# Two attention and mixture-of-experts layers in one kernel: the second attention's paddings written by ACT in the routed units instead of by POOL, and seven of eight shared units in front of the routed ones instead of six

## The chip, the cores and the metric

The kernel runs on one NeuronCore of a Trainium2 chip. A core has five engines with a queue each: TensorE (PE in the profile) for matrix products, VectorE (DVE), ScalarE (ACT), GpSimd (POOL) and SyncE (SP, which here only issues transfers). They wait for each other by semaphores. The metric is the time on the device in microseconds (us); lower is better.

## The reference

Four blocks follow each other on x of 2 x 512 x 256 float32, each as `x = x + layernorm(block(layernorm(x)))`. Blocks 0 and 2 are attentions (the first linear, with 32 heads of 64; the second with softmax, 32 query and 8 key/value heads of 8). Blocks 1 and 3 are the mixtures of experts (MoE) that the change is about, cut to what they compute:

```python
x = hidden_states.reshape(-1, Dm)                 # 1024 tokens of 256
logits = x @ router_w                             # 8 experts
expert_idx = jnp.argmax(logits, axis=-1)
score = jax.nn.sigmoid(jnp.max(logits, axis=-1))
xs = x * score[:, None]
for e in range(n_experts):
    m = (expert_idx == e)[:, None]
    xe = jnp.where(m, xs, 0.0)
    h = jax.nn.silu(xe @ gate_w[e]) * (xe @ up_w[e])
    out = out + jnp.where(m, h @ down_w[e], 0.0)
shared = jax.nn.silu(x @ shared_gate_w) * (x @ shared_up_w) @ shared_down_w
return out + shared
```

## The kernel before

Everything stays in SBUF as 8 tiles of 128 tokens (NT = 8), apart from the rows that are sorted by expert through memory. Each engine's program is written out by hand, and the order in each queue is the order of the code.

A MoE block (l = 0 for block 1, l = 1 for block 3; `pe_moe`, `act_moe`, `dve_moe`, `pool_moe`, `sp_moe`) works like this. TensorE makes the router's logits, VectorE chooses an expert and a slot for each token, and POOL scatters the tokens' rows to `sorted_x` with eight indirect transfers (L618). VectorE then works out which expert each tile of 128 sorted rows belongs to, in a chain of small operations that ends with the casts `row` (L937) and `expert` (L939). SP reads `row` and fetches 15 tiles of sorted rows (NR = NT + E - 1 = 15) into `xg`, a ring of 8. TensorE reads `expert` and multiplies each tile by its expert's weights. Each routed tile of results is stored by POOL with an indirect transfer (L624); at the end SP loads all results as `y`, VectorE adds the shared expert's part `y_shared`, and the statistics and normalisation of the next block follow.

The products are made in NU = 23 units u, 15 routed and 8 shared (the shared expert on one of the 8 token tiles). Units 0 to NSF - 1 are shared, the next 15 routed, the rest shared again. With NSF = 6, units 6 to 20 are routed, 21 and 22 shared. A unit passes through these stages:
- routed only: TensorE transposes the rows (`turn_rows`, L1306) and ACT copies them (L1059)
- gate/up on TensorE (L1282 shared, L1289 routed)
- SiLU on ACT (L1046), the product h on VectorE (L865 shared, L867 routed)
- transposes of h on TensorE (`turn_h`, L1298), copied by ACT (L1052)
- down on TensorE (L1318), copied from PSUM by VectorE (L876) to `y_shared` or to a ring `yr` of 4, from which POOL stores.

Step i of the loop holds gate/up of unit i, the transposes of h of unit i - 1, the row transposes of the routed tile two units ahead (both of the first two in step NSF - 1), and down of unit i - 2. The last gate/up step changes places with the transposes of h before it, and the step behind the last routed unit holds two downs:

```python
            for i in range(3, NU + 1):
                if i == NU - 1:
                    turn_h(i - 1)
                if i < NU:
                    gate_up(i)
                if i != NU - 1:
                    turn_h(i - 1)
```

The h product just ahead of the chain of small operations is unit 2's (`gated(2)`); the h products of units 3 and on stand behind `expert`.

The second attention (block 2) keeps its heads in tiles with padded columns: `qs` and `ks` (32 columns a head, of which 24 to 31 are zero, or one at three of them in `ks`, before the row maxima are put in) and `vals` (a column of ones for the softmax's sum, zeros behind). `pool_l1` writes these paddings in block 1: POOL issues eight memsets behind its scatters, five of zeros with no wait between them, then three of ones. `L1_CONSTS` is the number of signals that ACT, VectorE and POOL wait for before they use the tiles in block 2. Between block 1 and block 2 TensorE runs `keep_warm(25, 2)` (L1128), 25 products that nobody uses, once the first y is made, and `keep_warm(5, 2)` when VectorE's statistics are there.

Of the kernel before, what the change touches and what calls it, by code (L numbers as in the profile page):

```python
# [25 lines left out]
ACT = mybir.ActivationFunctionType  # L26
AX = mybir.AxisListType

P = 128
B, S, D = 2, 512, 256  # L30
NT = B * S // P
TB = S // P
# [14 lines left out]
E, F = 8, 256  # L47
FC = F // P
NR = NT + E - 1
NSF = 6  # L50
NXG = 8
NU = NT + NR
REGION = B * S
# [3 lines left out]
def routed(u):  # L57

    return u - NSF if NSF <= u < NSF + NR else None


def shared_tile(u):
    return u if u < NSF else u - NR

NQ, NKV, HD = 32, 8, 8
# [3 lines left out]
HW = 32  # L71
NKT = B * NKV // GH
Q_AT, K_AT, LO_AT = (0, 1), (0, 2), (2, 1)
MAXAT, MAXN = 3 * HD, 3
VW = 32
# [4 lines left out]
def build(nc, a, out):  # L80
    ctx = ExitStack()
    with ctx:
        def sem(name):
            return ctx.enter_context(nc.semaphore(name))

        def at(name, shape, dt, where):

            n = 1
            for d in shape[1:]:
                n *= d  # L90
            size = n * (2 if dt == BF16 else 4)
            t = nc.alloc_sbuf_tensor_at(name, shape, dt, offset=where[0])
            where[0] += (size + 31) // 32 * 32
            assert where[0] <= LIMIT, (name, where[0], LIMIT, here[0])
            return t
# [16 lines left out]
        ones = at("ones", [P, P], F32, here)  # L112
# [26 lines left out]
        zeros = at("zeros", [P, D], F32, here)  # L139
# [41 lines left out]
        h = [at(f"h{i}", [P, F], F32, me) for i in range(2)]  # L181
# [28 lines left out]
        qs = [at(f"qs{b}", [P, TB, NQ, HW], F32, l1) for b in range(B)]  # L210
        ks = [at(f"ks{b}", [P, TB, NKV, HW], F32, l1) for b in range(B)]
        vals = at("vals", [P, NT, NKV, VW], F32, l1)
# [22 lines left out]
        consts = sem("consts")  # L235
# [49 lines left out]
        l1_consts, l1_ordered = sem("l1_consts"), sem("l1_ordered")  # L285
# [172 lines left out]
        N_CONSTS = 14  # L458
# [74 lines left out]
            nc.gpsimd.tensor_tensor(shift[of][:, sl], nmean[of][:, sl], rstd[of][:, sl],  # L533
                                    ALU.mult).then_inc(rstd_ready[of], 1)

        def pool_l1(pool):

            g = nc.gpsimd
            g.memset(vals[:], 0.0).then_inc(l1_consts, 1)
            for b in range(B):  # L540
                g.memset(ks[b][:, :, :, MAXAT:HW], 0.0).then_inc(l1_consts, 1)
                g.memset(qs[b][:, :, :, MAXAT:HW], 0.0).then_inc(l1_consts, 1)
            pool.wait_ge(l1_consts, 5)
            for b in range(B):
                g.memset(ks[b][:, :, :, MAXAT:MAXAT + MAXN], 1.0).then_inc(l1_consts, 1)
            g.memset(vals[:, :, :, HD:HD + 1], 1.0).then_inc(l1_consts, 1)

        L1_CONSTS = 8

        def order_heads(pool):  # L550

            g = nc.gpsimd
            pool.wait_ge(l1_loaded, 48)
            rows = [(wqkv[:, c], wqkv_in[:, c]) for c in range(KC)] + [(bqkv[:], bqkv_in[:])]
            for to, src in rows:
                for s_ in range(2):
                    cols = slice(s_ * NQ // 2 * HD, (s_ + 1) * NQ // 2 * HD)
                    g.tensor_copy(to[:, cols].rearrange("p (h r d) -> p r h d", r=GH, d=HD),
                                  src[:, cols].rearrange("p (r h d) -> p r h d", r=GH, d=HD)).then_inc(l1_ordered, 1)
                g.tensor_copy(to[:, NQ * HD:], src[:, NQ * HD:]).then_inc(l1_ordered, 1)  # L560
# [41 lines left out]
        def pool_moe(pool, l):  # L602
            g = nc.gpsimd

            g.iota(xn_id[:, :, D:D + 1].bitcast(U32), pattern=[[P, NT], [0, 1]], base=SORTED,
                   channel_multiplier=1).then_inc(numbered, 1)
            pool.wait_ge(numbered, l + 1)
            pool.wait_ge(zeroed, 32 * (l + 1))
            for half in range(2):
                sl = slice(half * TB, (half + 1) * TB)  # L610
                pool.wait_ge(xn_ready[half], (2 * l + 2) * TB)
                pool.wait_ge(score_ready[l], half + 1)
                g.tensor_scalar(xn_id[:, sl, D + 1:D + 2], half_score[:, sl].unsqueeze(2), 0.5, 0.5, ALU.mult,
                                ALU.add).then_inc(score_put[l], 1)
                pool.wait_ge(score_put[l], half + 1)
                pool.wait_ge(slot_ready[l], half + 1)
                for t in range(half * TB, (half + 1) * TB):
                    g.indirect_dma_start(sorted_x[l][:, :], bass.IndirectOffsetOnAxis(ap=slot[:, t:t + 1], axis=0),  # L618
                                         xn_id[:, t, :], None).then_inc(scattered[l], 16)
            if l == 0:  # L620
                pool_l1(pool)
            for r in range(NR):
                pool.wait_ge(yr_ready[l], NSF + r + 1)
                g.indirect_dma_start(routed_y[l][:, :], bass.IndirectOffsetOnAxis(  # L624
                    ap=xg[r % NXG][:, D:D + 1].bitcast(U32), axis=0), yr[r % 4][:], None).then_inc(yr_stored[l][r % 4], 16)
            if l == 0:
                order_heads(pool)
# [330 lines left out]
        def scalar_program(act):  # L958
# [23 lines left out]
            def complete(p):  # L982

                for t in range(NT):
                    if p == BLOCKS - 1:
                        act.wait_ge(last_summed, t + 1)
                        act.wait_ge(rstd_ready[1], 2 * (2 * p + t // TB + 1))
                    nc.scalar.activation(x[:, t, :], x[:, t, :], ACT.Identity,
                                         bias=shift[1][:, t:t + 1]).then_inc(x_summed, 1)
# [44 lines left out]
            turn(3, 0)  # L1034
            turn(3, 1)
            act_moe(act, 1, turn)
            complete(BLOCKS - 1)

        def act_moe(act, l, turn):
            def silu(u):  # L1040
                act.wait_ge(gu_made[l], u + 1)
                if u >= 2:
                    act.wait_ge(h_ready[l], u - 1)
                r = routed(u)
                kw = {} if r is None else dict(scale=xg[r % NXG][:, D + 1:D + 2])
                nc.scalar.activation(sg[u % 2][:], ps[2 + u % 2][:, 0:F], ACT.Silu, **kw).then_inc(silu_ready[l], 1)  # L1046

            def copy_h(u):
                act.wait_ge(hT_made[l], u + 1)
                if u >= 2:  # L1050
                    act.wait_ge(d_made[l], u - 1)
                nc.scalar.activation(hT[u % 2][:], ps[4 + u % 2][:, 0:F].rearrange("p (c n) -> p c n", c=FC),  # L1052
                                     ACT.Copy).then_inc(hT_ready[l], 1)

            def copy_rows(r):
                act.wait_ge(xgT_made[l], r + 1)
                if r >= 2:
                    act.wait_ge(gu_made[l], NSF + r - 1)
                nc.scalar.activation(xgT[r % 2][:], ps[r % 2][:, 0:D].rearrange("p (c n) -> p c n", c=KC),  # L1059
                                     ACT.Copy).then_inc(xgT_ready[l], 1)  # L1060

            def score(half):
                sl = slice(half * TB, (half + 1) * TB)
                act.wait_ge(best_ready[l], half + 1)
                nc.scalar.activation(half_score[:, sl], best[:, sl], ACT.Tanh, scale=0.5).then_inc(score_ready[l], 1)

            act.wait_ge(logits_made[l], 1)
            nc.scalar.activation(lgT[0][0:HC, :], ps[LOGIT_BANK[0]][0:HC, 0:2 * P], ACT.Copy).then_inc(lgT_ready[l], 1)
            silu(0)
            score(0)  # L1070
            silu(1)
            turn(2 * l + 1, 2)
            turn(2 * l + 1, 3)
            copy_h(0)
            copy_h(1)
            score(1)
            silu(2)
            for i in range(3, NU + 1):
                if i == NU - 1:
                    copy_h(i - 1)  # L1080
                if i < NU:
                    silu(i)
                if i != NU - 1:
                    copy_h(i - 1)
                for r in rows_at_unit(i):
                    copy_rows(r)

        def downs_at(i):

            last = NSF + NR - 1  # L1090
            return [i - 2] if i <= last else [last - 1, last] if i == last + 1 else [i - 1]

        def rows_at_unit(i):

            return [0, 1] if i == NSF - 1 else [i + 2 - NSF] if NSF <= i and i + 2 - NSF < NR else []

# [370 lines left out]
        def act_l1(act, normalise, turn_copy, complete):  # L1467
# [11 lines left out]

            act.wait_ge(l1_consts, L1_CONSTS)  # L1480
            for t in range(TB):
# [29 lines left out]
        def pool_l1_loop(pool, link):  # L1511
            g = nc.gpsimd
            pool.wait_ge(l1_consts, L1_CONSTS)
            for t in range(TB):
# [204 lines left out]
        def dve_l1(dve, link, mark, settle, y_tiles, close_stats, sum_x):  # L1719
            v = nc.vector  # L1720
            dve.wait_ge(l1_ordered, L1_ORDERED)
            dve.wait_ge(l1_consts, L1_CONSTS)

# [104 lines left out]
```

## Time and profile before

| | |
|---|---|
| median of 3 runs | 671.64 us (670.51 to 672.01) |
| the profiled execution | 669.68 us |
| its span in the trace | 667.8 us |
| mean granted TensorE clock | 0.986 |
| busy TensorE, VectorE, ACT, POOL | 92%, 61%, 49%, 32% |
| block 1 (MoE, l = 0) | about 254 to 350 us |
| block 3 (MoE, l = 1) | about 577 us to the end |

The profiled execution is one run under the profiler; all rows are from it. The share of an engine's busy time is over the whole span, and says little about a single stage. The granted clock is the share of full speed that TensorE was given: 1.00 is 2.4 GHz and 0.50 is 1.2 GHz. Ends of matrix products are modelled, so two that follow each other may overlap by up to 0.2 us in the rows; starts are the better measure.

### The profile page before, as it was taken

Reading aid. Unit: us, or ns where it says so; the run is one execution under the profiler, and the core shown is the slowest. Engines: PE = TensorE matmul, PEld = TensorE weight load, DVE = VectorE, ACT = ScalarE, POOL = GpSimd, SP = SyncE. Lnnn points to the kernel's source line nnn. Section 1 sums busy time; section 2 is a strip of 40 time slices with the busy share of each in tenths; the row PEclk is TensorE's granted clock in tenths of the full one; section 3 lists DMA queues with packets and bytes.
Section 4 is the critical chain, followed back from the end, with each engine's and each line's share of the span. In section 5 each row is a group of like instructions: output and inputs, shape, how many; then the busy total and the mean of one; then the engine's idle time right before and its main releaser. Section 6 shows DMA issues by size and latency. Waiting matters only on the chain.

```text
span 667.8 us, 11795 instructions
## 1 busy us (share of the span) xinstructions
PE 617.4 (92%) x4298; PEld 408.0 (61%) x4298; DVE 404.4 (61%) x929; ACT 325.1 (49%) x645; POOL 213.2 (32%) x312
## 2 busy tenths in 40 slices
PE   3999999999999988799978999999999999989990
PEld 2887887887888785366665544444444445546660
DVE  4526705632760587533366999989998954743336
ACT  4523423433332224133215589898988875523322
POOL 5870561282073154513333031201010100331331
PEclk9999999999999999899989999999999999999996
DMA  6000200300199992222379994000000000031213
GB/s 220 33 1 33 96 1 20 107 1 1 38 283 299 78 314 77 78 58 81 105 237 346 303 180 3 1 1 2 2 1 2 1 2 1 9 104 55 81 56 126
DMA packets 69000, 57.40 MB, mean 86 GB/s; under 512 B 21520, under 2 KB 64400, under 8 KB 68944
## 3 DMA queue, kind: packets, MB, share of 16 engines
q1 hardware_dynamic: 66736, 50.60, 31.2%
q0 software_dynamic: 2208, 6.05, 2.5%
q8 instruction: 36, 0.59, 0.4%
q14 instruction: 20, 0.16, 0.1%
HBM read 30.78 MB, written 25.85 MB: 85 GB/s over the span
## 4 chain that ended last, share of the span: by engine, by line
PE 73%; DVE 16%; DMA 3%; ACT 3%; issue 2%; POOL 1%; SPq 1%; ACTq 0%; POOLq 0%; DVEq 0%
PE psum L303 9%; PE psum L305 8%; PE psum L304 8%; PE psum L1289 8%; PE psum L1634 8%; DVE mx L1744 7%; PE psum L1606 5%; PE psum L1318 5%; PE psum L1594 5%; PE psum L1619 3%; PE psum L1213 2%; DVE stat L666 2%; PE psum L1564 2%; PE psum L1282 2%; PE psum L1199 1%
## 5 line engine op out<-in xcount | busy, mean ns | idle before, releaser
L1744 DVE TENSOR_REDUCE mx<-psum 128x1 f32<-128x512 f32 x256 | 157.6, 681 | 17.6 <-PE psum L1606 17.5
L1505 ACT ACTIVATE pr<-psum 128x512 f32<-128x512 f32 x256 | 138.0, 598 | 27.9 <-PE psum L1619 26.1
L1634 PE MATMUL psum<-pr,vals 128*32 128x256 f32 x1024 | 77.6, 389 | 0.0
L1619 PE MATMUL psum<-qT,kT 32*128 32x512 f32 x256 | 76.6, 494 | 0.7 <-ACT pr L1505 0.7
L1606 PE MATMUL psum<-kT,qT 32*128 32x512 f32 x256 | 67.7, 488 | 1.7 <-ACT qT L1472 0.7
L1289 PE MATMUL psum<-w_gu,xgT 128*128 x120 | 56.4, 592 | 0.0
L624 POOL DMA_INDIRECT routed_y<-yr,xg x30 | 28.7, 958 | 86.1 <-DVE yr L876 85.5
L1606 PEld LDWEIGHTS psum<-kT,qT 32*128 32x128 f32 x256 | 26.3, 181 | 43.9 <-issue 21.4
L1546 POOL CAST mp<-mx 128x16 bf16<-128x16 f32 x16 | 3.1, 196 | 150.5 <-DVE mx L1744 150.5
L867 DVE SCALAR_TENSOR_TENSOR h<-psum,xg,sg 128x256 f32<-128x256 f32 x30 | 14.5, 484 | 49.8 <-ACT sg L1046 49.8
L1046 ACT ACTIVATE sg<-psum,xg 128x256 f32<-128x256 f32 x30 | 14.2, 474 | 60.4 <-PE psum L1289 60.4
L1013 ACT ACTIVATE q<-psum 128x512 f32<-128x512 f32 x32 | 19.1, 597 | 48.9 <-PE psum L305 48.9
L1634 PEld LDWEIGHTS psum<-pr,vals 128*32 128x32 f32 x1024 | 22.2, 108 | 29.8 <-issue 17.8
L585 POOL TENSOR_TENSOR ksum_t<-k_hi 128x1024 f32<-128x1024 f32 x8 | 19.2, 2401 | 64.6 <-DVE k_lo L814 64.4
L1619 PEld LDWEIGHTS psum<-qT,kT 32*128 32x128 f32 x256 | 34.4, 181 | 8.9 <-ACT pr L1505 4.0
L1019 ACT ACTIVATE q_hi<-q 128x512 fp32r<-128x512 f32 x32 | 20.2, 633 | 40.1 <-DVE q L845 40.1
L303 PE MATMUL psum<-kvo_hi,q_hi 128*128 128x256 f32 x128 | 38.0, 297 | 1.9 <-POOL q_lo L599 1.9
L531 POOL TENSOR_TENSOR rstd<-var,mhalf 128x4 f32<-128x4 f32 x16 | 16.5, 1028 | 64.8 <-DVE nmean L676 64.8
L304 PE MATMUL psum<-kvo_lo,q_hi 128*128 128x256 f32 x128 | 36.1, 282 | 0.0
L305 PE MATMUL psum<-kvo_hi,q_lo 128*128 128x256 f32 x128 | 36.1, 282 | 0.0
L819 DVE TENSOR_TENSOR nk<-psum,same_head 128x8 f32<-128x8 f32 x16 | 1.9, 161 | 53.0 <-PE psum L1191 53.0
L814 DVE SCALAR_TENSOR_TENSOR k_lo<-psum,k_hi 128x512 fp32r<-128x512 f32 x32 | 22.0, 689 | 18.1 <-ACT k_hi L1007 18.0
(214 smaller groups left out, 1406.6 us busy)
## 6 DMA issues: line engine op xcount, KB each, us to landing
sorted_x<-zeros SPq DMA_DIRECT2D x2, 9088.0 KB, 39.2
w_gu<-in_L_ffn_gate_w SPq DMA_DIRECT2D x16, 256.0 KB, 6.2
w_gu<-in_L_ffn_up_w SPq DMA_DIRECT2D x16, 256.0 KB, 6.3
w_d<-in_L_ffn_down_w SPq DMA_DIRECT2D x16, 256.0 KB, 6.6
xg<-sorted_x SPq DMA_DIRECT2D x30, 129.0 KB, 2.2
wk_f<-in_L_attn_Wk SPq DMA_DIRECT2D x4, 512.0 KB, 5.2
wq_f<-in_L_attn_Wq SPq DMA_DIRECT2D x4, 512.0 KB, 6.0
wv_f<-in_L_attn_Wv SPq DMA_DIRECT2D x4, 512.0 KB, 3.7
```

Of the source, the lines that this page charges most:

```text
L303: nc.tensor.matmul(o, lhs[0], rhs[0], start=start, stop=False, **kw)
L304: nc.tensor.matmul(o, lhs[0], rhs[1], start=False, stop=False, **kw)
L305: return nc.tensor.matmul(o, lhs[1], rhs[0], start=False, stop=stop, **kw)
L624: g.indirect_dma_start(routed_y[l][:, :], bass.IndirectOffsetOnAxis(ap=xg[r % NXG][:, D:D + 1].bitcast(U32), axis=0), yr[r % 4][:], None). ...
L1289: last = mm(ps[2 + u % 2][:], xgT[r % 2][:, c], w_gu[:, bass.ds(experts[r], 1), c, :], start=(c == 0), stop=(c == KC - 1))
L1318: last = mm(ps[6 + u % 2][:, 0:D], hT[u % 2][:, c], w, start=(c == 0), stop=(c == FC - 1))
L1505: nc.scalar.activation(pr[d % 3][:, j], s2_bank(d, j), ACT.Exp, scale=SCALE).then_inc(exp_ready, 1)
L1594: last = nc.tensor.transpose(into[:, t * P:(t + 1) * P], src, ident[:])
L1606: mm(s1_bank(c, j), qT1[n % 2][rows, t * P:(t + 1) * P], kT[n // GH][rows, :], start=True, stop=True).then_inc(s1_made, 1)
L1619: mm(s2_bank(d, j), kT[n // GH][rows, kc * P:(kc + 1) * P], qT2[n % 2][rows, :], start=True, stop=True).then_inc(s2_made, 1)
L1634: last = mm(ps[AV_BANK][j * VW:(j + 1) * VW, cols], vals[:, n // NKV * TB + kc, n % NKV // GH * GH + j, :], pr[d % 3][:, j, cols], start=( ...
L1744: v.tensor_reduce(mx[n % 2][:, t, j:j + 1], s1_bank(c, j), AX.X, ALU.max, negate=True).then_inc(max_read, 1)
```

## The change

`NSF` becomes 7: units 0 to 6 are shared, 7 to 21 routed, 22 shared, in both MoE blocks and on all engines. `pool_l1` is removed. In block 1 ACT writes the paddings with activations that copy a constant (`put`), one piece in each of the units 9 to 15, behind that unit's other work: n = 0 and 1 write the zeros of `qs` (128 x 1024 elements), 2 and 3 those of `vals` (128 x 736), 4 and 5 those and the ones of `ks` (128 x 160 and 128 x 96), 6 the ones of `vals` (128 x 64). That is nine activations, so `L1_CONSTS` becomes 9. The parts of `vals` that are overwritten later are no longer zeroed.

```diff
-NSF = 6
+NSF = 7
...
-        def pool_l1(pool):
-
-            g = nc.gpsimd
-            g.memset(vals[:], 0.0).then_inc(l1_consts, 1)
-            for b in range(B):
-                g.memset(ks[b][:, :, :, MAXAT:HW], 0.0).then_inc(l1_consts, 1)
-                g.memset(qs[b][:, :, :, MAXAT:HW], 0.0).then_inc(l1_consts, 1)
-            pool.wait_ge(l1_consts, 5)
-            for b in range(B):
-                g.memset(ks[b][:, :, :, MAXAT:MAXAT + MAXN], 1.0).then_inc(l1_consts, 1)
-            g.memset(vals[:, :, :, HD:HD + 1], 1.0).then_inc(l1_consts, 1)
-
-        L1_CONSTS = 8
+        L1_CONSTS = 9
...
-            if l == 0:
-                pool_l1(pool)
...
+        def put(act, to, value):
+            src = (zeros, ones)[value]
+            nc.scalar.activation(to, src[:, 0:1].unsqueeze(2).to_broadcast([P, to.shape[1], to.shape[2]]),
+                                 ACT.Copy).then_inc(l1_consts, 1)
+
+        def l1_padding(act, n):
+            heads = "p t h w -> p (t h) w"
+            if n == 0:
+                act.wait_ge(consts, N_CONSTS)
+            if n < 2:
+                put(act, qs[n][:, :, :, MAXAT:HW].rearrange(heads), 0)
+            elif n < 4:
+                put(act, vals[:, (n - 2) * TB:(n - 1) * TB, :, HD + 1:VW].rearrange(heads), 0)
+            elif n < 6:
+                put(act, ks[n - 4][:, :, :, MAXAT + MAXN:HW].rearrange(heads), 0)
+                put(act, ks[n - 4][:, :, :, MAXAT:MAXAT + MAXN].rearrange(heads), 1)
+            elif n == 6:
+                put(act, vals[:, :, :, HD:HD + 1].rearrange(heads), 1)
...
                 for r in rows_at_unit(i):
                     copy_rows(r)
+                if l == 0 and i > NSF + 1:
+                    l1_padding(act, i - NSF - 2)
```

## Rows read from the trace of the kernel before

**Rows 1.** The page's fourth part: shares of the chain that ended last, by engine.

```profile
PE 73%; DVE 16%; DMA 3%; ACT 3%; issue 2%; POOL 1%; SPq 1%; ACTq 0%; POOLq 0%; DVEq 0%
```

**Rows 2.** The chain of waits in the first MoE block: start, duration, what.

```profile
269.32 0.42 DVE h L865
...
272.88 4.73 DVE expert L939
...
283.36 0.44 PE psum L1306 x2
```

**Rows 3.** The chain of waits in the second MoE block.

```profile
588.46 0.42 DVE h L865
...
592.02 0.34 DVE expert L939
...
598.10 0.44 PE psum L1306 x2
```

**Rows 4.** Timeline of POOL, both blocks: start, duration, engine, line, operation.

```profile
272.50 0.96 POOL L618 DMA_INDIRECT sorted_x<-xn_id,slot  x1 [0.30 <-issue]
273.46 1.82 POOL L539 MEMSET vals<- 128x2048 f32 x1
...
276.60 0.97 POOL L542 MEMSET qs<- 128x1024 f32 x1
...
591.42 0.96 POOL L618 DMA_INDIRECT sorted_x<-xn_id,slot  x1 [0.30 <-issue]
```

**Rows 5.** Timeline of TensorE where the routed units start, first and second block.

```profile
281.88 0.38 PE L1298 MATMUL psum<-ident,h 128*128 128x128 f32 x2
...
284.50 1.88 PE L1289 MATMUL psum<-w_gu,xgT 128*128 x4
...
595.46 0.38 PE L1298 MATMUL psum<-ident,h 128*128 128x128 f32 x2
...
598.37 1.03 PE L1318 MATMUL psum<-shared_d,hT 128*128 128x256 f32 x4
599.24 1.88 PE L1289 MATMUL psum<-w_gu,xgT 128*128 x4
```

**Rows 6.** Timeline of the first block's end; idle time and releaser in brackets.

```profile
326.55 1.88 PE L1289 MATMUL psum<-w_gu,xgT 128*128 x4
...
328.27 0.38 PE L1298 MATMUL psum<-ident,h 128*128 128x128 f32 x2
...
328.49 1.03 PE L1318 MATMUL psum<-w_d,hT 128*128 x4
...
328.98 0.48 DVE L867 SCALAR_TENSOR_TENSOR h<-psum,xg,sg 128x256 f32<-128x256 f32 x1 [1.80 <-ACT sg L1046]
...
331.29 1.91 PE L1318 MATMUL psum<-w_d,hT 128*128 x8
...
332.36 0.42 DVE L876 COPY yr<-psum 128x256 f32<-128x256 f32 x1 [0.24 <-PE psum L1318]
...
340.63 7.48 PE L1128 MATMUL psum<-ident 128*128 128x128 f32 x50 [2.53 <-DVE y L953]
...
348.67 1.38 PE L1128 MATMUL psum<-ident 128*128 128x128 f32 x10 [0.57 <-DVE nmean L676]
...
350.86 1.82 PE L1111 MATMUL psum<-ident,xn_id 128*128 128x128 f32 x8 [0.81 <-ACT xn_id L979]
```

**Rows 7.** ACT's strided copies (ns min/median/max), and a SiLU of a routed unit.

```profile
L1457 ACT ACTIVATE ks<-qkv x4: 293/301/309, 356.1 to 358.8; 128x128 fp32r<-128x128 f32 x4
L1457 ACT ACTIVATE qs<-qkv x4: 614/614/615, 356.3 to 359.0; 128x512 fp32r<-128x512 f32 x4
...
292.46 0.47 ACT L1046 ACTIVATE sg<-psum,xg 128x256 f32<-128x256 f32 x1 [2.00 <-PE psum L1289]
```

**Rows 8.** TensorE in two stretches: length, busy (instructions), granted clock, DMA share, GB/s.

```profile
277.60:280.00 2.40, 2.32 (x7) 0.50 0.00 0
...
344.60:345.60 1.00, 1.00 (x8) 0.65 0.90 268
```

## The prediction

> **What bounds the kernel now.** I read the page first, then the chain of waits around each mixture-of-experts (MoE) block, then the timelines of the engines there. The chain is TensorE's for 73% and VectorE's for 16%, and POOL and ACT together have 4% [rows 1]. So an edit on POOL or ACT counts only where TensorE or VectorE waits for it, and an edit of TensorE's order only where it moves a wait.
>
> The kernel runs the same MoE code twice, and only the first run has POOL's paddings in it, so the second is a control. Line the two up at VectorE's h product: 269.32 [rows 2] and 588.46 [rows 3], 319.14 us apart. The cast of `expert` starts at 272.88 and at 592.02, again 319.14 apart. It takes 4.73 us in the first block and 0.34 in the second. The second pair of row transposes, which waits for the rows that SP fetches by the table, starts at 283.36 and at 598.10: only 314.74 apart. So the first block loses 319.14 - 314.74 = 4.40 us at this cast, all of it on the chain, because the first routed gate/up product comes at 284.50 against 599.24, also 314.74 apart [rows 5].
>
> What holds a cast of 16 elements? POOL's timeline [rows 4]: its last scatter runs from 272.50 to 273.46, and behind it five memsets without a wait in between, from 273.46 to 276.60 + 0.97 = 277.57. The cast ends at 277.61, right after the fifth. In the second block the last scatter runs to 592.38 and the cast ends at 592.36. The reader is to see that VectorE's cast comes back when POOL's uninterrupted stretch ends, in both blocks.
>
> The Trainium skill, SBUF — State Buffer, Who interferes with whom, has a rule for this: GpSimd and VectorE share one pair of ports as an exclusive lock, casts and copies can need it, and whoever comes second is blocked for the whole instruction of the other. The trace agrees that the cast is blocked, and differs in the length: one memset's lock would be over at 275.28 and the memsets would have cost 1.82 us of the hold; the trace shows 277.61, after five. What follows if the rest is not the memsets' is the second rival.
>
> **Part 1: POOL's eight memsets go.** With them the cast's hold ends as in the second block. The first block then runs at the second's times less 319.14: -4.40 us at the first routed product. Not all of the hold goes: the scatter stays, and it ends at 273.46, where the second block's less 319.14 would be 273.24. So the cast, and the h product that follows it in order on VectorE and restarts TensorE, may come up to 0.22 later than the control says. The bounds are 0 and 0.22; I take 0.2, since the second block's cast ended with its scatter. POOL itself has only the row stores behind the memsets, which wait for the routed rows, so it gains nothing of its own.
>
> **Part 2: ACT writes the paddings.** Nine activations in seven units of the first block. The nearest rows are ACT's strided copies into the same tiles in the same runs of 8 elements [rows 7]: 0.301 us for 128 elements per partition, 0.614 for 512, so 0.82 ns an element. For `qs` (1024 elements): 0.614 + 512 x 0.00082 = 1.03 us, twice. For `vals` (736): 0.80, twice. For `ks` (160 and 96 elements): about 0.33 + 0.28 = 0.61, twice. For the ones of `vals` (64): 0.25. In all 5.1 us of ACT, one piece per unit, behind that unit's last copy. ACT is idle 2.00 us there in each routed unit before TensorE gives it the next SiLU [rows 7], so I cost it at nothing. Bounds: below, nothing; above, every element at the small row's 0.301/128 = 2.35 ns gives 2.4 us for 1024, 0.4 over the idle time in two units. Behind the piece stand the next SiLU and two copies. The product of SiLU is needed by TensorE only one unit later: it is ready 2.91 us after the gate/up product starts (326.55 to 328.98 + 0.48), and is transposed a routed unit and a gate/up later, (2.81 + 0.22) + 1.72 = 4.75 after that start (part 3). So 1.8 us more of cover stands behind the 2.00, and the upper bound is nothing too. Who waits for the paddings: POOL, VectorE and ACT at the second attention's start, while the last is written in unit 15 of 23.
>
> **Part 3: one shared unit moves ahead of the routed ones, in both blocks.** Its own time on TensorE: 1.72 for gate/up (326.55 to 328.27), 0.22 for the transposes of h, 0.87 for down (598.37 to 599.24) = 2.81 us [rows 5, 6]. What it hides, in the second block: between the transposes of h at 595.46 and down at 598.37 there are 2.91 us, and own work there is one pair of transposes of h and two of rows, 3 x 0.22 = 0.66. So 2.25 us are waiting for rows. The unit fills all of it and sticks out by 2.81 - 2.25 = 0.56: the first routed product goes from 599.24 to 599.80. The rows must be there by then: TensorE comes to the second pair at 598.71, and they were there at 598.10. In the first block, less 319.14, it comes at 279.57 and they are there 5.75 after the cast (277.61 to 283.36), at 273.45 + 5.75 = 279.20: hidden too. So the first block starts its first routed product at 599.80 - 319.14 = 280.66 instead of 284.50: -3.84, with the 0.2 of part 1 it is -3.64.
>
> No instruction is added to a queue: the fetches on SP, the weights and the 15 row stores on POOL keep their order. The fetch ring needs stores only eight rows back, which move with the products.
>
> **The end of a block.** The time that counts is when the last two routed rows leave PSUM, since the stores, the loads of y and the next normalisation hang on them; the shared units behind were hidden by that. Before: last routed product at T = 326.55, downs 19 and 20 from T + 4.74 = 331.29, first copy at 332.36 [rows 6]. After: the unit behind the last routed one is now the last of all, whose step transposes first, then multiplies. TensorE is there at T + 2.81, h is ready at T + 2.91, and with a few hundredths for the semaphore that is 0.15 of waiting (an estimate); then 0.22, 1.72, and the two downs at T + 4.90. That is +0.15 in each block. The final shared down ends far ahead of the loads of y: before, two shared units ended 2.53 us ahead of the restart, now one.
>
> **The sum.** First block -3.64 + 0.15 = -3.49. Second block +0.56 + 0.15 = +0.71. Net -2.78, with bounds -2.98 (no rest of the hold) and -2.76. The profiled execution took 669.68 us (span 667.8, 1.88 outside it): 666.9 by this. The median of the runs is 671.64, 1.96 above it; the difference carries over, so 671.64 - 2.8 = 668.8.
>
> **Rivals.** *The hold stays* (slower, 5%). If the cast waits for something other than memsets, for example the eight scatters' descriptors, only the order changes. Then TensorE in the first block goes on from 281.88 (transposes of h) with 0.22 + 0.87 + 1.72 + 0.22 + 0.44 + 0.87 = 4.34, to 286.22 instead of 284.50: +1.72, +0.15 at the end, and +0.71 in the second block: +2.6, 674.2 us. It decides from a rest of the hold of about 3 us on. Against it: the same scatters stand in the second block, and the cast took 0.34.
>
> *A colder clock in front of the second attention* (4%). With one shared unit less behind, TensorE idles 2.53 + 2.81 = some 5.3 us before its warming matmuls at 340.63. The granted clock already falls in them: of 344.6 to 345.6 seven tenths are still at 1.2 GHz (0.65 granted), so it is back at 2.4 some 4.7 us after the restart; after the stall of the cast it was at 1.2 from 277.6 to 280 [rows 8]. The 50 records took 7.48 us; at 2.4 GHz throughout, 0.11 each, they would take 5.5, wholly at 1.2 GHz 10.9. They have 7.48 + 0.57 before the next ones are due, and 0.81 more stand behind those [rows 6]. With cold stretches as long as seen, up to 4.7 us from the start on, they take 5.5 + 2.35 = 7.8: nothing lost. Only if the clock stayed down throughout: 10.9 - 8.05 - 0.81 + 1.1 for the ten cold ones = 3.1, and +0.3 in all, 671.9. The Trainium skill, TensorE: Matmul & The Clock Gate, What's actually happening, says that the idle state is the throttled one and activity releases it; both rises here agree.
>
> *A part of the hold stays* (6%). If only one memset's length was the memsets' doing and the rest of the hold is the last scatter's own, the cast ends at 277.61 - 1.82 = 275.79. TensorE restarts there instead of at 273.4, 2.4 later than in the forecast, and the rows come at 281.5, hidden by the same shift: -3.84 + 2.4 + 0.15 + 0.71 = -0.6, 671.1 us. For it: the rule above. Against it: the second block's cast was free 0.02 before its scatter's end.
>
> *ACT becomes the bound* (2%): a padding over 3.8 us. At 5 us each for the wide ones it is 4 x 1.2 = +4.8 less 2.8, 673.6; no row is near it.
>
> **Chances and range.** Forecast 82%, with a range of its own of 667.6 to 669.8 (the bounds, and some 0.75 us on either side, half of what the runs before spread), and 1% for what I don't see. The rivals lie above and hold 17%, so this range alone would leave out a little more than 2 in 10; 667.0 to 670.6 allows for twice that spread. I count 0.2% (1.3 us) as what a measurement can tell from no change. Faster: the forecast and the lucky ends of the rivals, 0.84; same: the part of the hold and the clock, 0.08; slower: the hold and ACT, 0.08.
>
> **What would show it.** Right: the cast of `expert` near 0.3 to 0.6 us in the first block; no TensorE idle of 4 us and no 1.2 GHz there; first routed product 11.3 to 11.5 us after the h product in both blocks (15.18 and 10.78 before); no waiting for rows in front of the row transposes; the last downs 4.90 after the last routed product starts; ACT's nine pieces in its idle time. Wrong: a cast that stays long, row transposes that still wait, or warming matmuls that end after VectorE's statistics.

## The result, and the profile after

The changed kernel takes 666.27 us in the median of 20 runs (665.17 to 670.84), the kernel before 672.15 in the median of 20 (669.33 to 677.79): ratio 0.9908, 95% interval 0.989 to 0.9926. It is faster, by twice what was forecast, and under the range of 667.0 to 670.6. (Of all runs below, one of `before_delay_9` stands apart, 1933.37 us at a mean granted clock of 0.292; that kernel's median is of its other eleven.)

The profiled executions differ by less: 665.62 against 669.68 us. VectorE's timeline of the changed kernel, with the cast of `expert` in the first block and in the second (start, duration, engine, line):

```profile
268.34 0.42 DVE L851 TENSOR_TENSOR h<-sg,psum 128x256 f32<-128x256 f32 x1 [1.71 <-ACT sg L1051]
...
271.90 0.18 DVE L925 CAST expert<-expert_f 128x16 int32<-128x16 f32 x1
272.01 0.42 DVE L851 TENSOR_TENSOR h<-sg,psum 128x256 f32<-128x256 f32 x1
...
587.16 0.33 DVE L925 CAST expert<-expert_f 128x16 int32<-128x16 f32 x1
```

POOL's timeline over the same cast, with nothing behind the last scatter until the first row store:

```profile
271.51 0.96 POOL L606 DMA_INDIRECT sorted_x<-xn_id,slot  x1 [0.30 <-issue]
289.62 0.96 POOL L610 DMA_INDIRECT routed_y<-yr,xg  x1 [17.16 <-DVE yr L862]
```

The cast took 4.73 us before [rows 2] and takes 0.18 now, in the middle of a scatter: the scatter does not hold it. TensorE's timeline where the routed units start, first and second block, and at the first block's end:

```profile
278.14 0.38 PE L1305 MATMUL psum<-ident,h 128*128 128x128 f32 x2
278.36 0.60 PE L1313 MATMUL psum<-ident,xg 128*128 128x128 f32 x4
278.80 1.03 PE L1325 MATMUL psum<-shared_d,hT 128*128 128x256 f32 x4
279.66 1.88 PE L1296 MATMUL psum<-w_gu,xgT 128*128 x4
...
593.62 0.60 PE L1313 MATMUL psum<-ident,xg 128*128 128x128 f32 x4
594.06 1.03 PE L1325 MATMUL psum<-shared_d,hT 128*128 128x256 f32 x4
594.93 1.88 PE L1296 MATMUL psum<-w_gu,xgT 128*128 x4
...
321.71 1.88 PE L1296 MATMUL psum<-w_gu,xgT 128*128 x4
...
324.68 0.44 PE L1305 MATMUL psum<-ident,h 128*128 128x128 f32 x2
...
326.68 1.89 PE L1325 MATMUL psum<-w_d,hT 128*128 x8
```

No wait stands in front of the row transposes any more. ACT's paddings, one unit, and the groups for the four shapes (ns min/median/max):

```profile
288.25 0.39 ACT L1064 ACTIVATE xgT<-psum 128x256 f32<-128x256 f32 x1
288.52 1.06 ACT L1027 ACTIVATE qs<-zeros 128x1024 f32<-128x1024 f32 x1
290.64 0.47 ACT L1051 ACTIVATE sg<-psum,xg 128x256 f32<-128x256 f32 x1 [1.06 <-PE psum L1296]
...
L1027 ACT ACTIVATE vals<-zeros x2: 825/826/827, 294.6 to 297.6; 128x736 f32<-128x736 f32 x2
L1027 ACT ACTIVATE ks<-zeros x2: 373/376/378, 300.6 to 303.6; 128x160 f32<-128x160 f32 x2
L1027 ACT ACTIVATE ks<-ones x2: 278/280/283, 300.8 to 303.8; 128x96 f32<-128x96 f32 x2
```

For what follows, each trace is cut at five starts: h of unit 2 (H), the first routed gate/up (R), the first y (Y), the first scores of the second attention (S), and H, R, Y again in block 3. The stretches, in us, each the difference of two starts:

| kernel | start to H | H to R | R to Y | Y to S | S to H | H to R | R to Y |
|---|---|---|---|---|---|---|---|
| before | 269.32 | 15.18 | 55.65 | 22.04 | 226.27 | 10.78 | 55.32 |
| changed | 268.34 | 11.32 | 55.59 | 22.06 | 226.29 | 11.33 | 55.65 |
| difference | -0.98 | -3.86 | -0.06 | +0.02 | +0.02 | +0.55 | +0.33 |

From block 1 on that is -3.00 us. The 0.98 us lie ahead of everything that the change touches; in the traces of the other kernels below H comes at 268.2 to 269.6 with POOL's memsets and at 268.3 to 269.7 with ACT's paddings, so they belong to the execution. Then 1.9 us are still missing from the 5.9 of the medians. The profiled execution of the kernel before lies 2.5 us under its median, that of the changed kernel 0.65.

### The profile page after: what moved, and what is told of

Its sections match the earlier page's. It is cut to its first block, busy times and chain, and to the rows that moved or that the text cites. A ratio compares the mean times of both kernels' runs of the same rounds, so it can differ in the third digit from the quotient of the medians.

```text
span 663.9 us, 11796 instructions
## 1 busy us (share of the span) xinstructions
PE 615.3 (93%) x4298; PEld 407.6 (61%) x4298; DVE 400.0 (60%) x929; ACT 328.4 (49%) x654; POOL 208.7 (31%) x304
## 4 chain that ended last, share of the span: by engine, by line
PE 76%; DVE 15%; ACT 3%; DMA 2%; issue 2%; POOL 2%; ACTq 0%; POOLq 0%; SPq 0%; DVEq 0%
PE psum L303 9%; PE psum L305 9%; PE psum L304 9%; PE psum L1296 8%; PE psum L1641 8%; DVE mx L1751 7%; PE psum L1325 5%; PE psum L1613 5%; PE psum L1601 5%; PE psum L1626 3%; PE psum L1289 3%; DVE stat L652 2%; PE psum L1220 2%; PE psum L1571 2%; PE psum L1305 1%
```

## The experiments

**The change taken apart: `pads_only`, `order_only`.** The changed kernel with the old order, and the kernel before with the new order.

```diff
pads_only (from the changed kernel)
-NSF = 7
+NSF = 6
order_only (from the kernel before)
-NSF = 6
+NSF = 7
```

> The changed kernel with six shared units in front, as before: only POOL's paddings go to ACT. My sum: the cast of expert takes 0.2 to 0.3 us, first routed product 10.8 to 11.0 us after the h product in both blocks (15.18 in the first before); the profiled execution 4.4 us under the kernel before, and 1.5 us under the changed kernel (no +0.56 and no +0.15 to 0.22 in either block). The rival, that the order brought the part of the gain that I did not forecast: only 1 to 3 us under the kernel before, and over the changed kernel.

> The kernel before with seven shared units in front, memsets still on POOL behind the scatters. My rival's sum: the cast still takes 4.7 us, first block +1.72 + 0.2, second +0.56 + 0.2, so 2.6 us over the kernel before. If the order brought part of the gain, it is the same or faster.

Measured: `pads_only` 668.19 us (ratio 0.9936, 0.9907 to 0.9966), `order_only` 673.45 (1.0018, 0.9992 to 1.0044), beside 672.28 of the kernel before. In their traces the first block does what the sums say: H to R is 10.87 us in `pads_only` (cast 0.17) and 16.96 in `order_only` (cast 4.71), where the prediction's rival had 15.18 + 1.72 = 16.90 for the case that the hold stays. So the gain in the rows is the hold's. But the medians do not add up: -4.1 and +1.2 make -2.9, which is the forecast, and both together bring -5.9. And `pads_only` is 1.9 us slower than the changed kernel where the rows say 1.4 faster. Both traces have something that neither the trace of the kernel before nor that of the changed kernel has, a stretch at 1.2 GHz in the second attention. TensorE in `pads_only` around it (stretch, length, busy, instructions, granted clock, DMA share, GB/s), then the same place of the attention in the kernel before:

```profile
376.00:379.90 3.90, 3.34 (x17) 1.00 1.10 337
380.00:386.70 6.70, 6.59 (x44) 0.50 1.13 264
386.90:392.00 5.10, 5.10 (x56) 1.00 1.28 195
```

```profile
380.00:384.50 4.50, 3.95 (x18) 1.00 1.10 333
384.60:391.30 6.70, 6.59 (x72) 1.00 1.11 278
```

In equal time TensorE gets through 44 records instead of 72. S to H is 228.93 and 229.02 us in the two traces instead of 226.3: such a stretch costs 2.7. Ahead of it TensorE was busy for 3.34 of 3.90 us; the largest gap, 0.52 us, is a wait for ACT's exponentials. The kernel before waits there for 0.51 us, and its clock stays at 2.4 GHz.

**What holds the cast: `memsets_late`, `memsets_apart`.** The kernel before, with the same memsets behind a wait for the casts, or each with a wait behind it.

```diff
memsets_late
-            if l == 0:
-                pool_l1(pool)
             for r in range(NR):
+                if l == 0 and r == 0:
+                    pool.wait_ge(expert_ready[l], 2)
+                    pool_l1(pool)
memsets_apart (in pool_l1)
             g.memset(vals[:], 0.0).then_inc(l1_consts, 1)
+            pool.wait_ge(l1_consts, 1)
             for b in range(B):
                 g.memset(ks[b][:, :, :, MAXAT:HW], 0.0).then_inc(l1_consts, 1)
+                pool.wait_ge(l1_consts, 2 * b + 2)
                 g.memset(qs[b][:, :, :, MAXAT:HW], 0.0).then_inc(l1_consts, 1)
-            pool.wait_ge(l1_consts, 5)
+                pool.wait_ge(l1_consts, 2 * b + 3)
```

> The kernel before with the same eight memsets on POOL, but behind a wait for the two table casts. If POOL's stretch holds only the casts and not VectorE's products and copies out of PSUM: the cast takes 0.2 to 0.3 us, the h products and copies keep 0.42, and the gain is that of pads_only, 4.4 us in the profiled execution, with no work on ACT. If every VectorE operation is held while POOL writes: an h product of about 4 us just behind the cast, and no gain.

> The kernel before with POOL waiting for its own signal after each of the five first memsets. If the hold of VectorE's cast lasts as long as POOL's uninterrupted stretch: the cast ends with the scatter or the first memset, after 0.6 to 2.5 us instead of 4.72, and the first routed product comes 11 to 13.5 us after the h product. If every further memset takes the port again before VectorE gets it: 4.7 us or a little more, as before.

`memsets_late` took 668.49 us (0.994, 0.9916 to 0.9964), as `pads_only`, with H to R at 10.89 and no work on ACT. Its VectorE and POOL in one list:

```profile
272.06 0.96 POOL L618 DMA_INDIRECT sorted_x<-xn_id,slot  x1 [0.30 <-issue]
...
272.45 0.17 DVE L940 CAST expert<-expert_f 128x16 int32<-128x16 f32 x1
...
273.02 1.82 POOL L539 MEMSET vals<- 128x2048 f32 x1
...
273.41 0.42 DVE L866 TENSOR_TENSOR h<-sg,psum 128x256 f32<-128x256 f32 x1
274.38 0.42 DVE L877 COPY y_shared<-psum 128x256 f32<-128x256 f32 x1 [0.55 <-PE psum L1319]
```

The first memset starts at the scatter's end, 0.40 us behind the cast's, and an h product and a copy out of PSUM run under it at their usual 0.42: of what VectorE does here only the cast is held, and with it what stands behind it in VectorE's order. `memsets_apart` (one execution, 668.83):

```profile
272.19 2.43 DVE L941 CAST expert<-expert_f 128x16 int32<-128x16 f32 x1
...
272.77 1.82 POOL L539 MEMSET vals<- 128x2048 f32 x1
274.65 0.31 POOL L542 MEMSET ks<- 128x256 f32 x1
```

The cast ends at 274.62, just behind the first memset (272.77 + 1.82 = 274.59), and H to R is 12.94: a wait between the memsets alone gives 2.24 us back. (The time of the whole shows less of it, because this trace has the 1.2 GHz stretch in the attention: S to H is 228.91.) So the hold lasts as long as POOL works without a wait, and the prediction's reading of [rows 4] stands. The Trainium skill, SBUF — State Buffer, Who interferes with whom, gives the hold the length of one instruction; that is so in this run, and not where the next memset has nothing to wait for.

**Is it the stall's cold clock? `warm_stall`.** 18 unused products in TensorE's 4.3 us of waiting for the cast, in the kernel before.

```diff
                 if i != NU - 1:
+                    if l == 0 and i == 4:
+                        keep_warm(18, 0)
                     turn_h(i - 1)
```

> The kernel before with 18 unused products on TensorE in the 4.3 us in which it waits for the cast; the hold itself stays. Theory A, that the runs of before spread (669.3 to 677.8) because the clock falls in this stall and stays down for a stretch that differs from run to run: the granted clock stays at 1.00 there, the spread shrinks to some 1.5 us and the median comes down by 1.5 to 3 us to 669 to 670.5. Theory B, that the spread comes from elsewhere (loads at the start, the clock before the second attention): the median and the spread stay as before within 0.1%.

672.63 us (1.0002, 0.9972 to 1.0031), spread 669.2 to 677.1: nothing gained. In its trace the clock falls all the same, at the wait for rows (282.46, where it was 277.03 before), and H to R is 16.30 instead of 15.18. Theory A fell in this form; filling one wait moved the fall to the next.

**Keeping the attention warm: `before_warm`, `after_warm`, `pads_warm`.** Eight more unused products in steps 6 and 7 of the second attention, four in front of score products of the kind shown and four, by the same two lines, in front of those of the other kind.

```diff
                     wait_bank(pe, ("s1", c * GH + j))
+                    if c in (6, 7) and j == 2 * i:
+                        mm(s1_bank(c, j)[:, 0:P], ident[:], ident[:], start=True, stop=True)
```

> The kernel before with eight unused products more on TensorE in steps 6 and 7 of the second attention, where the profiled executions of pads_only and order_only show the clock at 1.2 GHz for 6.8 us and the stretch from the first scores to block 3 at 228.9 to 229.0 us instead of 226.3. Theory A: most executions of the kernel before have this fall, its profiled one had not; kept warm, the median comes down from 672.2 by some 2 us to 670, and the mean clock of most runs goes from 0.978 to 0.982 or more. Theory B: the fall is not what lifts the median of before over its profile; the median stays within 0.7 us of before, and the clocks as they are.

> The changed kernel with the same eight unused products. Its runs are mostly at a mean clock of 0.983 with 13.4 us of it in the idle time before the attention and at the end, so theory A gives it nothing: 666.3 within 0.7. If it gains 2 us too, the fall is as frequent there and does not explain the difference of the medians.

> Paddings on ACT, six shared units in front, and the unused products. By the sums of the blocks it is 1.4 us under the changed kernel once the clock does not fall in the attention: 665.0. If pads_only's 668.2 stays, the fall is not what sets its median.

675.19, 671.82 and 672.99 us beside 671.66 of before. These say nothing for either theory, because the products are not free: with no fall at all in the attention of `after_warm`'s trace, S to H is 229.40 instead of 226.29. I had taken those steps to be VectorE's; the added 3.1 us show that they have no slack on TensorE. The traces of `before_warm` and `pads_warm` have the fall as well, at 27.0 and 25.6 us behind S (the start of the first scores).

**Does the place of the attention matter? `delay_3`, `delay_5`, `delay_8`, `delay_10`.** The changed kernel with 3, 5, 8 or 10 unused VectorE operations in front of block 1's first y.

```diff
+            dve.wait_ge(gathered[0][0], 16)
+            for _ in range(3):
+                link(v.tensor_tensor(past[:], past[:], past[:], ALU.max))
             y_tiles(1, range(0, 2), moe_y)
```

> The changed kernel with three unused VectorE operations, each waited for, in front of the first y of block 1: everything behind is about 1.0 us later and nothing else changes. Theory A, that the median depends on where the second attention falls against the moments at which TensorE's clock is set anew, so that a shift alone brings or avoids a fall: the medians of the four shifts over 666.3 plus their shift differ from each other by 1.5 us or more. Theory B, that a fall is a matter of chance, the same for every shift: each is 666.3 plus its shift within 0.5, here 667.3.

> As delay_3 with five operations, about 1.6 us. Theory A: from the profiled executions, this brings the attention to where pads_only, order_only and memsets_apart had the fall, so this is the one most likely over its shift: 667.9 plus up to 2.6. Theory B: 667.9.

> As delay_3 with eight operations, about 2.6 us. Theory A: between delay_5 and delay_10. Theory B: 668.9.

> As delay_3 with ten operations, about 3.3 us. Theory A: the stretches at 1.2 GHz in the traces are 3.41 us or twice that long, so a shift of about that much brings the attention back to where it was: 669.6 within 0.7, with most runs at the changed kernel's mean clock. Theory B: 669.6 as well; so only the middle ones tell them apart.

| | added (trace) | median | over 666.27 plus the added | S to H in the trace |
|---|---|---|---|---|
| delay_3 | 1.01 | 668.80 | +1.5 | 227.74 |
| delay_5 | 1.66 | 670.07 | +2.1 | 227.71 |
| delay_8 | 2.64 | 671.60 | +2.7 | 228.94 |
| delay_10 | 3.30 | 669.98 | +0.4 | 226.24 |

B's 0.5 us is passed three times: with five and eight operations the intervals (ratios 0.9957 to 0.9996 and 0.9968 to 1.0006) lie wholly above the changed kernel's moved by the added time, with three they overlap a little. So a shift can cost more than its length. That ten operations are 1.6 us faster than eight is what theory A says, but it isn't shown: ten have 0.9957 to 1.0, nearly the interval of eight. The three with an excess have the stretch at 1.2 GHz in the attention of their trace, 22.4 to 23.8 us behind S, and the fourth has not. TensorE in `delay_8`:

```profile
379.00:382.70 3.70, 3.15 (x16) 1.00 1.13 304
382.80:389.50 6.70, 6.67 (x47) 0.50 1.12 248
```

**Can work be added for nothing? `pads_delay_2`, `before_delay_9`, `mixed`, `before_a`.** The same edit with 2 operations in `pads_only` and 9 in the kernel before; the changed kernel with seven shared units in front in block 1 and six in block 3; and the kernel before once more.

```diff
mixed
-NSF = 7
+NSFS = (7, 6)
...
-    return u - NSF if NSF <= u < NSF + NR else None
+    return u - NSFS[l] if NSFS[l] <= u < NSFS[l] + NR else None
```

> pads_only with two unused VectorE operations (0.7 us) in front of the first y of block 1. In pads_only the second attention begins 0.7 us sooner after block 1's h product than in the changed kernel. Theory A (alignment): the added work brings it to where the changed kernel has it, the fall goes, and the kernel is faster than without the added work: by the blocks' sums 666.3 - 1.5 + 0.7 = 665.5, within 0.8, against 668.2 of pads_only. Theory B (no alignment): 668.2 + 0.7 = 668.9.

> The kernel before with nine such operations (2.9 us). Its attention lies 3.9 us behind the changed kernel's, 0.5 over the 3.41 of a stretch at 1.2 GHz; 2.9 more makes it twice 3.41. Theory A: the fall that lifts its median goes and the added 2.9 us cost nothing or little: 672.2 to 673.0. Theory B: 672.2 + 2.9 = 675.1.

> Paddings on ACT, seven shared units in front in block 1 (so that the attention lies where the changed kernel has it) and six in block 3, where the seventh cost 0.55 + 0.33 us in the profiled execution. Theory A: 666.3 - 0.9 = 665.4, under both kernels. Theory B, that the seventh unit in block 3 has a part in the low median: 666.3 or more.

> One more execution of the kernel before with its trace. Theory A: if its time is 671.5 or more, there is a stretch at 1.2 GHz in the second attention that the profiled execution of before (669.68) has not, with 1.3 to 2.7 us more from the first scores to block 3's h product than 226.3. Theory B: the time over 669.7 lies elsewhere.

668.28 us (0.9946, 0.9923 to 0.9969), 674.37 (1.0027, 1.0001 to 1.0054), 667.23 (0.9928, 0.9905 to 0.9951), and one execution of 669.95. The 0.7 us in `pads_delay_2` cost 0.1; the 2.9 in `before_delay_9` cost 2.2 to 2.4. Each lies between the theories and nearer to B's number. `mixed` lies 1.8 us over A's number and has B's outcome: by its rows it should be 0.7 us faster than the changed kernel, and its median is 1.0 slower. So the place of the attention is not all. The execution `before_a` doesn't meet theory A's condition of 671.5 and settles nothing, but it had the fall, 23.6 us behind S, with S to H at 227.76; its time was low because H came 1.1 us earlier than in the other.

A fall can also come late in the attention. TensorE in `before_delay_9`, 182 us behind S:

```profile
540.00:546.90 6.90, 6.34 (x64) 1.00 0.01 2
547.10:557.20 10.10, 10.10 (x51) 0.50 0.01 2
```

S to H is 230.64 there, 4.4 us too long. `memsets_late` has a fall at the same place, for a third of that time, with 227.64. Yet another place shows in `pads_delay_2`, TensorE around the wait for rows in block 1, then in block 3:

```profile
277.43 0.44 PE L1316 MATMUL psum<-ident,xg 128*128 128x128 f32 x2 [1.51 <-DMA xg<-sorted_x]
278.30 0.44 PE L1316 MATMUL psum<-ident,xg 128*128 128x128 f32 x2 [0.44 <-DMA xg<-sorted_x]
278.58 1.03 PE L1328 MATMUL psum<-shared_d,hT 128*128 128x256 f32 x4
279.44 3.57 PE L1299 MATMUL psum<-w_gu,xgT 128*128 x4
...
596.02 0.44 PE L1316 MATMUL psum<-ident,xg 128*128 128x128 f32 x2 [1.71 <-DMA xg<-sorted_x]
596.66 0.47 PE L1316 MATMUL psum<-ident,xg 128*128 128x128 f32 x2 [0.20 <-issue]
596.93 1.90 PE L1328 MATMUL psum<-shared_d,hT 128*128 128x256 f32 x4
598.63 2.74 PE L1299 MATMUL psum<-w_gu,xgT 128*128 x4
```

Gate/up takes 3.57 instead of 1.88 and down 1.90 instead of 1.03. The clock fell right behind the wait for rows, in both blocks; H to R and R to Y of block 3 are 11.70 and 57.04 instead of some 10.9 and 55.3, 2.5 us. (This trace has the fall in the attention too, 22.7 us behind S.) `before_warm` has a fall in block 3 as well (at 603.8, H to R 11.95, R to Y 55.99). These are 2 of the 11 traces that have the wait for rows in block 3 unfilled. In the traces with seven units in front, where that wait is gone, H to R of block 3 is 11.32 or 11.33 in all seven. None of 7 against 2 of 11 is too little to show that the fall goes with the wait.

**Filling the wait for rows: `rows_warm`, `before_rows_warm`.** Seven unused products inside the wait, in `pads_only` (both blocks) and in the kernel before (block 3).

```diff
                     turn_h(i - 1)
+                if i == NSF - 1:
+                    keep_warm(7, 0)
                 for r in rows_at_unit(i):
```

> pads_only with seven unused products on TensorE (some 1.5 us) inside its wait for the first sorted rows in both MoE blocks. Theory C, that with six shared units in front this wait lets the clock fall in many executions, and the seventh unit is worth what it saves there: the median comes from 668.2 to 666.5 or less, and the first routed product still comes 10.9 us after the h product. Theory A alone (only the alignment of the attention counts): 668.2 within 0.7.

> The kernel before with the same seven products in block 3 alone, where it waits 2.25 us for the rows. Theory C: 1 to 1.5 us under before, 670.7 to 671.2. Theory A alone: as before, 672.2 within 0.7.

`before_rows_warm` took 670.63 us beside 672.15 of the kernel before (0.9987, 0.996 to 1.0013), `rows_warm` 667.37 (0.993, 0.9904 to 0.9955; `pads_only` had 668.19). Both medians move down, by 1.5 and 0.8; the first is theory C's number, the second falls between C and A. The first's interval includes no change, and the second's overlaps that of `pads_only` (0.9907 to 0.9966). The products do fit into the wait (H to R 10.98 and 10.69 in `rows_warm`). Its trace has other falls, one in front of the attention (Y to S 23.86 instead of 22.06) and two in it, 2.7 and 26.5 us behind S (S to H 230.85).

## Why the prediction was wrong

**The hold of the cast.** Right, and it is the cause of what the rows gain: `pads_only` and `memsets_late` bring it by two ways, `memsets_apart` half of it. H to R is -3.86 where -3.64 was forecast: the rest of 0.2 that I left to the scatter isn't there. The rival in which the scatter's own work is a part of the hold fell with it.

**ACT's paddings.** Right. 1.06, 0.83, 0.38 + 0.28 and 0.32 us against 1.03, 0.80, 0.61 and 0.25, and the next SiLU starts as punctually as before, with 1.06 of the 2.00 us still idle.

**The seventh unit.** In an execution without a fall it costs what was worked out: +0.55 in block 3 against +0.56, and in block 1 of `order_only` 16.96 - 15.18 = +1.78 for a stall that stays, against 1.72. The end of a block was sized low: the last downs start at T + 4.97 (326.68 - 321.71) instead of T + 4.90, and VectorE puts the last h product in front of the copy; block 3's R to Y is +0.33 instead of +0.15. In block 1 it is -0.06, with the first load of y shorter in that execution (2.91 against 3.19 us).

**The colder clock in front of the attention.** The clock did fall in the longer idle time, earlier and for 6.8 us instead of 3.4, and it cost nothing: Y to S is 22.06 against 22.04.

**The step that failed** is the last of the sum, "the difference carries over". The terms give -2.78, and the profiled executions, with the start taken off, -3.00. But the 1.96 us between the profiled execution of before and its median were not an offset that both kernels share. The executions of a kernel differ in whether and where TensorE's clock falls, and with the change their mix is another: the median lies 2.5 us over the profiled execution before and 0.65 after. The mean granted clock of the single runs shows it. Of 147 runs of the kernel before that were taken beside the experiments, only 13 have 0.984 or more (median 669.5 us); 59 have 0.978 (672.4) and 17 have 0.973 (675.3). Of the changed kernel's 20, 15 have 0.983 (666.16). The profiled execution of before, at 0.986, was one of the few in the fast group, and from fast group to most frequent group the change brings 3.3 us, near the 3.00 of the rows. The rest of the 5.9 comes from the kernel before being seldom in its fast group.

The traces show three places where a fall costs time:
- In the second attention some 23 us behind S, behind a stretch in which TensorE is not quite busy: 1.4 to 2.7 us (S to H 227.7 to 229.0 against 226.3). The delay series shows that a mere shift can bring it, with an excess of up to 2.7 us in the median.
- In the second attention 182 us behind S: 1.4 and 4.4 us in two traces.
- Behind the wait for rows: 2.5 us in block 3 of one trace. The seventh unit removes that wait; that it removes the falls there isn't shown. I had counted the 2.25 us of waiting [rows 5] at their own length, and by that the unit could only lose.

A fourth place costs little. The clock also falls behind the held cast, in the traces of the kernel before for 3.4 us (H to R 15.18) or for 6.8 (15.54 in `before_a`), but H to Y is 70.82 and 70.84 us in these two.

The range went wrong with the same step: it took half of the 1.5 us that three runs of before had spread, and 20 runs spread 8.5.

**What stays open.** Why the kernel before has costly falls more often than the changed one, and how the missing 3 us are shared between these places. A mean clock doesn't say where a fall lies. The medians put the value of the seventh unit beyond its rows at 3.3 us with ACT's paddings and about 1.2 with POOL's; filling the wait gave 0.8 and 1.5. Since a shift alone can move the median by up to 2.7 beyond its length, these differences of medians can't be told apart from shifts, and I have one trace of each kernel, two of the kernel before. Why `mixed`, whose attention lies within 0.1 us of the changed kernel's, and `pads_delay_2`, for which the sums say the same, have 1.6 and 2.8 us of excess where that has none, is not explained either. In the trace of `pads_delay_2` the attention does not lie there: the fall in block 1 puts it 1.7 us later. None of the versions beats the changed kernel in the median; the lowest single runs are `pads_only`'s 664.98 and `rows_warm`'s 665.06 against 665.17.

## What to carry to other kernels

One profiled execution is one draw. Where its time stands well off the median of the runs, the mean granted clock of the single runs should be asked for before a sum is carried over, and the result of a small edit is not its own unless a pure shift of the same length has been tried. A wait of TensorE can cost more than its length, where the clock falls behind it, so useful work moved into it can be worth more than the rows of one execution say. Small casts and copies on VectorE that a chain hangs on should not meet an unbroken run of POOL operations; a wait between those, or a place behind the casts, is enough.

## What the runs showed of the hardware

The cast in the kernel before started at 272.88, 0.58 us ahead of the first memset's recorded start of 273.46, and was held nevertheless, while the same cast 0.39 us into a scatter took 0.17 (`memsets_late`) and 0.18 us (changed kernel) without memsets that could follow at once. So a memset that waits for nothing can hold a cast that the profile shows as started before it. Whether the hold begins early or the memset's recorded start is late, these rows don't tell.

VectorE's rows behind a held cast look long too (4.61, 4.27 and 3.77 us in the kernel before, 2.33, 1.99 and 1.48 in `memsets_apart`): they are recorded from their usual starts and all end within 0.01 us of the cast. With the hold gone they take 0.42.

The granted clock of TensorE fell from 1.00 to 0.50 after stretches that were mostly busy, 3.34 of 3.90 us in `pads_only`, and not only after idle ones, and the same stretch passed without a fall in the kernel before (3.95 of 4.50 us).
